# Other orders of work for layer 2 of a four-layer graph network kernel, on one core

## The reference

```python
qkv = (h @ W).reshape(Bn, Nn, 3, H, HEAD_DIM).transpose(2, 0, 3, 1, 4)
q, k, v = qkv[0], qkv[1], qkv[2]
mask = jnp.where(adj == 0, -jnp.inf, 0.0)
scores = jnp.einsum('bhid,bhjd->bhij', q, k) / np.sqrt(HEAD_DIM) + mask
out = jnp.einsum('bhij,bhjd->bhid', softmax(scores), v)
```

## Time and profile before

| | |
|---|---|
| median of 3 runs | 976.77 us (974.41 to 977.3) |
| the profiled execution's own time | 974.33 us |
| its span, first to last instruction | 972.3 us |
| TensorE busy | 904.8 us (93%) |
| VectorE, ScalarE, GpSimd busy | 641.8, 511.6, 382.1 us |
| mean granted TensorE clock | 0.965 of full speed |

### The profile page before, as it was taken

The page is one execution under the profiler, slowest core; times in us unless marked ns, Lnnn a source line. Parts: engine busy times, 40 slices in busy tenths (PEclk is TensorE's granted clock), DMA queues, the critical chain, the costliest instruction groups (busy, mean ns, idle before and its releaser), DMA issues. The chain is left out here.

```text
span 972.3 us, 20901 instructions
## 1 busy us (share of the span) xinstructions
PE 904.8 (93%) x6004; PEld 642.1 (66%) x6020; DVE 641.8 (66%) x1944; ACT 511.6 (53%) x919; POOL 382.1 (39%) x433
## 2 busy tenths in 40 slices
PE   6999999999999699976489999999999998999996
PEld 5799999999999688732255444455444443677775
DVE  4754554554554676556366777677776774899997
ACT  4323121121121336564356777777777757888884
POOL 4011021021020130000246777777777766355554
PEclk9999999999999899988579999999999999999999
DMA  8000000000000100000133343333343331011111
GB/s 243 23 12 12 12 23 12 11 22 11 22 0 0 35 9 0 0 1 1 33 66 66 67 90 86 81 69 65 67 92 81 84 77 25 1 33 32 32 32 43
DMA packets 34235, 40.66 MB, mean 42 GB/s; under 512 B 6672, under 2 KB 17552, under 8 KB 34192
## 3 DMA queue, kind: packets, MB, share of 16 engines
q1 hardware_dynamic: 32816, 39.87, 17.1%
q10 hardware_dynamic: 1376, 0.27, 0.1%
HBM read 6.43 MB, written 4.19 MB: 11 GB/s over the span
## 5 line engine op out<-in xcount | busy, mean ns | idle before, releaser
L1756 DVE CUSTOM_DVE_ANT_0 junk<-bank,mask_ij 128x512 bf16<-128x512 f32 x256 | 166.4, 688 | 69.2 <-PE bank L1839 61.1
L1617 POOL TENSOR_TENSOR half_sum<-prob 128x1024 f32<-128x1024 f32 x64 | 151.8, 2381 | 30.1 <-ACT prob L1692 29.9
L1692 ACT ACTIVATE prob<-wide 128x1024 f32<-128x1024 f32 x128 | 126.8, 1017 | 54.7 <-PE wide L1856 54.7
L431 ACT CAST yT<-wide 128x512 fp32r<-128x512 f32 x48 | 28.2, 589 | 206.1 <-PE wide L827 156.8
L531 POOL TENSOR_TENSOR Xr<-Xf,Xr 128x512 fp32r<-128x512 f32 x16 | 20.4, 1291 | 168.2 <-ACT Xr L426 167.9
L1839 PE MATMUL bank<-qkT 32*128 32x512 f32 x256 | 75.5, 513 | 6.6 <-DVE mx L1756 5.3
L1839 PEld LDWEIGHTS bank<-qkT 32*128 32x128 f32 x256 | 31.2, 187 | 70.8 <-DVE mx L1756 46.0
L1852 PE MATMUL wide<-qk_st 128*128 128x512 f32 x256 | 76.1, 419 | 0.0
L1439 PEld LDWEIGHTS bank<-Wh,pr 128*128 128x128 f32 x512 | 65.3, 191 | 13.7 <-ACT pr L1292 5.3
L59 PE MATMUL bank<-z,L3T_hi 128*128 128x256 f32 x256 | 73.9, 289 | 0.0
L60 PE MATMUL bank<-z,L3T_hi 128*128 128x256 f32 x256 | 73.6, 287 | 0.0
(11 more groups left out here) (299 smaller groups left out, 2285.3 us busy)
## 6 DMA issues: line engine op xcount, KB each, us to landing
qk_st<-qkT SPq DMA_DIRECT2D x192, 128.0 KB, 2.4
out_dram<-rc SPq DMA_DIRECT2D x15, 256.0 KB, 2.3
Xf<-X SPq DMA_DIRECT2D x14, 256.0 KB, 2.3
A<-in_adj_dram SPq DMA_DIRECT2D x4, 256.0 KB, 4.6
qk_st<-neg_row SPq DMA_DIRECT2D x64, 2.0 KB
Xf<-in_x_dram SPq DMA_DIRECT2D x2, 256.0 KB, 7.1
mask_q<-mask_ji SPq DMA_DIRECT2D x16, 32.0 KB, 1.8
w<-in_L_gnn_W_dram SPq DMA_DIRECT2D x2, 128.0 KB, 2.2
```

What stands on the lines that cost most here:

```text
L1617: pool.tensor_tensor(flat(half_sum[h][:]), flat(prob[bp][h][:, 0:2]), flat(prob[bp][h][:, 2:4]), ALU.add).then_inc(h_sum, 1)
L1692: act.activation(flat(prob[bp][h][:, 2 * half:2 * half + 2]), wide[half][:], ACT.Exp, scale=SCALE).then_inc(t_exp, 1)
L1756: dve.tensor_tensor_reduce(out=junk[hh][:], in0=bank[4 + hh][:], in1=m.mask_ij[:, i], scale=1.0, scalar=3.0 * MASKED, op0=ALU.add, op1=ALU ...
```

## The change

All five lists of layer 2 are replaced. The new lists begin at another place of the same cycle, so most stage numbers differ by one without the piece being done in another place. What stands elsewhere in the cycle is this:

- TensorE: before, `t0 D0 s0 m D1 V0 s1 t1 V1 s2 x V2 V3 s3 t2`; after, `t0 s0 m D0 D1 V0 V1 s1 t1 s2 V2 V3 s3 x t2`. T stands after s5 and ahead of q, no longer after t3.
- ScalarE: nr ahead of E4 and no longer behind it; kh behind vc and no longer ahead of it; N between mr and E1 and no longer behind E5.
- VectorE: R ahead of ql; u7 ahead of kl, where kl stood ahead of u7.
- GpSimd: r ahead of S2, where it stood behind it.
- SyncE: for a batch, dn1 st0 dn0 st1 dn3 dn2 st2 st3 without another batch's pieces between them; before, st0 of a batch stood ahead of st2 and st3 of the one before, and dn1 and dn0 behind st1.
- At the border to layer 3 the loops run a step further and the lists of `tail` begin that much later. TensorE's m.15 stands ahead of 3x.0 and D0.14, no longer between D0.14 and D1.14. GpSimd's constants and first copy come later in its order, and S3.14 stands ahead of r.13 (behind it before).

```diff
-        PE_ORDER = staged("V0:4 s1:2 t1:3 V1:4 s2:2 x:1 V2:4 V3:4 s3:2 t2:3 s4:2 n:2 d:4 o:4 s5:2 q:1 t3:3 T:0 s6:2 k:1 "
-                          "v:2 s7:2 t0:2 D0:3 s0:1 m:2 D1:3")
-        ACT_ORDER = staged("y:5 f:4 xh:1 xc:1 E4:3 nr:2 E5:3 N:0 qh:1 E6:3 E7:3 kh:1 vc:2 E0:2 mr:2 E1:2 e:3 Y:0 E2:2 E3:2")
-        DVE_ORDER = staged("u5:2 ql:1 R:0 u6:2 kl:1 u7:2 B:0 u0:1 b:4 u1:1 u2:1 u3:1 u4:1 c1:3 c2:3")
-        POOL_ORDER = staged("S3:3 g1:0 g2:4 S0:2 S1:2 xl:0 S2:2 r:3 X:0")
-        SP_ORDER = staged("st3:2 dn3:2 st1:1 dn1:1 dn0:1 st0:0 st2:1 dn2:1")
+        PE_ORDER = staged("t0:3 s0:2 m:3 D0:4 D1:4 V0:4 V1:4 s1:2 t1:3 s2:2 V2:4 V3:4 s3:2 x:1 t2:3 s4:2 n:2 d:4 o:4 "
+                          "s5:2 T:0 q:1 t3:3 s6:2 k:1 v:2 s7:2")
+        ACT_ORDER = staged("kh:2 E0:3 mr:3 N:0 E1:3 Y:1 e:4 E2:3 E3:3 y:5 f:4 xh:1 xc:1 nr:2 E4:3 E5:3 qh:1 E6:3 E7:3 vc:2")
+        DVE_ORDER = staged("u5:2 R:0 ql:1 u6:2 u7:2 kl:1 B:0 u0:1 b:4 u1:1 u2:1 u3:1 u4:1 c1:3 c2:3")
+        POOL_ORDER = staged("xl:1 r:4 S2:3 X:1 S3:3 g1:0 g2:4 S0:2 S1:2")
+        SP_ORDER = staged("st3:1 dn1:0 st0:0 dn0:0 st1:0 dn3:0 dn2:0 st2:0")
...
-            run(pool, POOL_ORDER, work, last=15)
+            run(pool, POOL_ORDER, work, last=16)
             third.pool_constants(pool)
-            tail("S3.13 g2.12", POOL_ORDER, work, None)
             third.pool_copy(pool, 0, 0, first=True)
-            tail("S0.14 S1.14 S2.14 r.13 S3.14 g2.13 S0.15 S1.15", POOL_ORDER, work, None)
+            tail("S2.14 S3.14 r.13 g2.13 S0.15 S1.15", POOL_ORDER, work, None)
...
-            run(act, ACT_ORDER, work, last=16)
+            run(act, ACT_ORDER, work, last=17)
             item = third.act_items(act)
-            tail("y.12 f.13 E4.14 nr.15 E5.14 E6.14 E7.14 vc.15 E0.15 3XR.0 mr.15 E1.15 3X.0 e.14 E2.15 E3.15 y.13 f.14 E4.15 "
...
+            tail("E0.15 3XR.0 mr.15 E1.15 3X.0 e.14 E2.15 E3.15 y.13 f.14 E4.15 E5.15 3W0.0 3W1.0 E6.15 E7.15 3XR.1 3G.0 3L0.0 "
...
-            run(pe, PE_ORDER, work, last=16)
+            run(pe, PE_ORDER, work, last=17)
             item = third.pe_items(pe)
             pe.wait_ge(third.const, 3)
-            tail("V0.13 s1.15 t1.14 V1.13 s2.15 V2.13 V3.13 s3.15 t2.14 s4.15 n.15 d.13 o.13 s5.15 t3.14 s6.15 v.15 s7.15 t0.15 "
-                 "3x.0 D0.14 m.15 D1.14 V0.14 t1.15 V1.14 3j.0 V2.14 V3.14 t2.15 d.14 o.14 3w0.0 3w1.0 t3.15 3i.0 3x.1 3j.1 D0.15 "
...
+            tail("t0.15 m.15 3x.0 D0.14 D1.14 V0.14 t1.15 V1.14 3j.0 V2.14 V3.14 t2.15 d.14 o.14 3w0.0 3w1.0 t3.15 3i.0 3x.1 3j.1 "
...
```

More of the change, by code:

```diff
@@ L1707, in work @@
                     act.copy(oT[:], ring["V0"][:]).then_inc(o_c, 1)
-            run(act, ACT_ORDER, work, last=16)
+            run(act, ACT_ORDER, work, last=17)
             item = third.act_items(act)
-            tail("y.12 f.13 E4.14 nr.15 E5.14 E6.14 E7.14 vc.15 E0.15 3XR.0 mr.15 E1.15 3X.0 e.14 E2.15 E3.15 y.13 f.14 E4.15 "
-                 "E5.15 3W0.0 3W1.0 E6.15 E7.15 3XR.1 3G.0 3L0.0 3L1.0 3X.1 3L2.0 e.15 3L3.0 y.14 3E0.0 f.15 3W0.1 3W1.1 3E1.0 "
-                 "3XR.2 3G.1 3L0.1 3L1.1 3X.2 3L2.1 y.15", ACT_ORDER, work, item)
+            tail("E0.15 3XR.0 mr.15 E1.15 3X.0 e.14 E2.15 E3.15 y.13 f.14 E4.15 E5.15 3W0.0 3W1.0 E6.15 E7.15 3XR.1 3G.0 3L0.0 "
+                 "3L1.0 3X.1 3L2.0 e.15 3L3.0 y.14 3E0.0 f.15 3W0.1 3W1.1 3E1.0 3XR.2 3G.1 3L0.1 3L1.1 3X.2 3L2.1 y.15", ACT_ORDER, work, item)
             pairs(act, B, 4, third.in_order(item, third.act_order), last=B, first=3)
@@ L1886, in work @@
                     last.then_inc(d_ps, 1)
-            run(pe, PE_ORDER, work, last=16)
+            run(pe, PE_ORDER, work, last=17)
             item = third.pe_items(pe)
             pe.wait_ge(third.const, 3)
-            tail("V0.13 s1.15 t1.14 V1.13 s2.15 V2.13 V3.13 s3.15 t2.14 s4.15 n.15 d.13 o.13 s5.15 t3.14 s6.15 v.15 s7.15 t0.15 "
-                 "3x.0 D0.14 m.15 D1.14 V0.14 t1.15 V1.14 3j.0 V2.14 V3.14 t2.15 d.14 o.14 3w0.0 3w1.0 t3.15 3i.0 3x.1 3j.1 D0.15 "
-                 "D1.15 V0.15 V1.15 V2.15 3q0.0 3q1.0 V3.15 3w0.1 3q2.0 3w1.1 3q3.0 d.15 o.15 3i.1 3x.2 3a0.0 3j.2 3a1.0 3q0.1 "
-                 "3q1.1 3a2.0", PE_ORDER, work, item)
+            tail("t0.15 m.15 3x.0 D0.14 D1.14 V0.14 t1.15 V1.14 3j.0 V2.14 V3.14 t2.15 d.14 o.14 3w0.0 3w1.0 t3.15 3i.0 3x.1 3j.1 "
+                 "D0.15 D1.15 V0.15 V1.15 V2.15 3q0.0 3q1.0 V3.15 3w0.1 3q2.0 3w1.1 3q3.0 d.15 o.15 3i.1 3x.2 3a0.0 3j.2 3a1.0 "
+                 "3q0.1 3q1.1 3a2.0", PE_ORDER, work, item)
             pairs(pe, B, 4, third.in_order(item, third.pe_order), first=3)
```

## The result

| | before | after |
|---|---|---|
| median, same chip | 976.73 us (974.41 to 977.3, 4 runs) | 970.62 us (969.82 to 971.99, 4 runs) |
| ratio with its 95% interval | | 0.9943 [0.9923, 0.9964] |
| the profiled execution's own time, span | 974.33, 972.3 us | 969.93, 968.0 us |
| mean granted TensorE clock | 0.965 | 0.965 |
| one step of the loop | 20.77 us | 20.44 us |

The account below looks back on a forecast made before the run. TensorE's sequence was taken to bound the kernel, at 20.77 us a step. Loop -2.1, fill -2.0 and border -0.1 summed to -4.2 us: 972.6 from a median of 976.8, range 968 to 978.

Parts of the forecast that it names:

- the loop: Layer 2's steady steps: -0.16 us a step over 13 steps, -2.1 us, bounds -3.4 to +1.8.
- the border: Where layer 3 begins: D0.14 and D1.14 joined, GpSimd's r.13 later; -0.1 us, between -0.3 and +0.5.
- the fill: Start of layer 2's pipeline: k no longer waits for ql, x moves behind s3; -2.0 us, between -0.6 and -3.
- Joined column tiles: TensorE's D0, D1, V0, V1 in one run: two junctions more at 0.12 us each, -0.24 us a step.
- The rival that joining saves nothing: Loads of all-row groups don't overlap, new neighbours bring nothing: step 21.0, total 977.7 us, no measurable change; chance 0.17.
- New neighbours of x and T: TensorE: t2 behind x saves 0.10 us a step, q behind T 0.05.
- Waits between scores and maxima: TensorE's score pairs waiting on VectorE: 0.36 us a step before, 0.54 after, +0.18.
- D0 behind kl: D0 follows k on its bank and waits for kl: covered by 0.07 us, +0.05 a step, bounds 0 and 0.2.
- GpSimd: r ahead of S2, X and S3 costs nothing, with 0.3 to 0.4 us of cover before D0 needs S3.
- The rival with a stall: GpSimd bounds the step because r ahead of S2 and S3 makes D0 wait: slower, above +2.9 us; chance 0.10.
- the third rival: The fill gives nothing because TensorE's clock falls again, and the loop alone pays: 974.1 us, about the same; chance 0.13.

Follow-up runs that it names:

- the split kernel: Changed kernel with D0 s0 m D1 V0 s1 t1 V1 ordered as before, each piece keeping the changed kernel's bank: 983.48 us, 1.0078 of the kernel before.
- the second pair: Both kernels executed once more with no edit: before 975.45 us (ratio 0.9994), after 971.22 us (ratio 0.996).

## Why the prediction was right, and which of its terms were off

The forecast lay 2 us above the median, on the right side of no change, and its range held the median. The mechanism in the loop was right. The sizes were not: the loop and the border gave 1.8 and 1.7 us more than forecast in the profiled execution, the fill 4.1 less, and these cancelled by luck.

*Joined column tiles*, forecast -0.24 us a step: measured 3.83 in before to 3.57, -0.26, and +0.27 when two junctions are taken away again. The rival that joining saves nothing is refuted. The weight loads show the overlap themselves: V0's first load runs at 642.24, while D1's last matmuls run until V0's first starts at 642.67.

```profile
642.24 0.14 PEld L1872 LDWEIGHTS bank<-prob,v 128*32 128x32 f32 x4 [0.29 <-issue]
```

(The Trainium skill, TensorE: Matmul & The Clock Gate, Part 3, The mechanism, lists that loads overlap matmuls in flight only where the row group differs, while its text ahead of the list also names a background weight buffer; the trace disagrees with the list for these all-row groups at different column tiles.)

*New neighbours of x and T*, forecast -0.10 and -0.05: this is the term of the step that was mis-sized. x took 0.59 us to V2, in front of all-row column tiles, and takes 0.41 in front of t2; t2 falls from 1.49 to 1.47. That is -0.20, and x put back costs it. T and q go from 0.59 + 0.81 to 0.53 + 0.80, -0.07 (653.69 to 654.22). I had looked for the saving in the full-height matmul behind the transpose, and it was in the transpose itself: what a piece takes to the next start depends on its successor as well. d, behind n, fell from 0.71 to 0.66, which wasn't forecast.

*Waits between scores and maxima*, forecast 0.36 to 0.54: measured 0.15 at s0, 0.16 at s2 and 0.29 at s5, 0.60 in all. s4 and s7 wait for nothing, as forecast. In every second step s7 takes 0.54 to 0.59 instead of 0.43, and then s0 waits less (0.43 to 0.49 instead of 0.59): one replaces the other. The body of the loop ends there, and s7 takes 0.43 where the loop is left, so I put it down to the loop's branch. That isn't shown: in before the body ends between D1 and V0, and D1 takes 0.88 to 0.89 in every step.

*D0 behind kl*, forecast +0.05: m to D0 goes from 0.20 to 0.27, +0.07. The bound of 0.2 wasn't reached, but the experiments show how near it is: with D0 a score pair and m earlier the wait is 0.66 us (the split kernel).

The step's sum, -0.26 - 0.20 - 0.07 - 0.05 + 0.24 + 0.07 = -0.27, comes within 0.06 of the measured -0.33. Averages over the loop's steps with complete records close the gap: the joined tiles give -0.28 (3.85 to 3.57), m to D0 +0.06, and v, which took 1.05 us in every second step of before and 0.98 in the others, takes 0.98 throughout: -0.03. Over the whole loop it is -3.93, where the forecast had -2.1: 1.8 us more, and outside the bounds given for it (-3.4 to +1.8).

*GpSimd*: the cover was forecast at 0.3 to 0.4 us and is 0.4. The rival with a stall never came near. Nor did t0 wait for a transfer in any step, and q (654.22) stood directly behind T; it waited for c2 once, 0.46 us at 776.88.

*The fill*, forecast -2.0. Its beginning went as forecast: counted from T of batch 0, s0 of batch 0 starts 1.85 us earlier (475.95 - 459.33 against 473.35 - 458.58; forecast 1.6) and t0 of batch 0 3.0 us. The term as a whole was borne out for the order itself (2.2 with the clock held up), and wrong for this execution (+1.4; -0.6 in the second pair; counted from T of batch 0, +2.1 and -0.2). That is the third rival's first half, TensorE's clock; the rival was too small in price, about 1.5 us, and I had argued that the new fill leaves no longer gap. It does: 1.90 us ahead of s1 of batch 1, where before's longest in the same place was 1.29. But closing that gap to 0.61 didn't keep the clock up, so the gap isn't the cause that it looks like. What is shown is that the clock costs the fill's gain; that adding matmuls brings it back; and that the clock is lower with this order than with before's: over 480 to 515 us it is 0.60 to 0.68 in the six traces whose fill has the new TensorE order, and 0.74 and 0.70 in before's two. Before loses by the clock too, only less: with the added matmuls t0 of batch 1 comes 4.3 to 6.0 us earlier in it, and 7.6 to 8.0 in after. (The Trainium skill, TensorE: Matmul & The Clock Gate, Part 1, HAM oscillation, tells of a kernel whose clock falls in waits for transfers and must be won back each time. Here the clock fell behind a wait for VectorE, but no run shows that the wait brought it down.)

*The border*, forecast -0.1: t0.15 to t3.15 goes from 13.27 to 12.95 us, -0.3, and about so in every other pair. The other -1.5 of the profiled pair lies in D0 and D1 of batch 15, behind the same waits, first before, then after:

```profile
822.73 3.40 PE L1864 MATMUL bank<-half_sum,ones_hd 128*32 128x512 f32 x16 [1.01 <-POOL half_sum L1617]
```

```profile
819.87 1.92 PE L1862 MATMUL bank<-half_sum,ones_hd 128*32 128x512 f32 x16 [1.00 <-POOL half_sum L1617]
```

Over the 10 us from there on the granted clock is 0.85 in before and 1.00 in after, but 0.72 and 0.85 in their second executions, where these matmuls take 3.64 and 3.35 us. The same order shows the fall once and once not, so I count the -1.5 as chance.

Open stays why the clock comes back at 500 us in the two traces with x ahead of V2 in the fill and only behind 505 us in those of the new order without it, and why it does so in some executions only. Before's fill has TensorE busy for only 2.59 of the 4 us from 496 to 500 and still has the full clock there, so a look at one gap doesn't settle it. Not tried: x early and the added matmuls together, and added matmuls at the border.

## What to carry to other kernels

Price a piece by the distance to the start of its successor and put it beside the successor it will have, not the one it had; a transpose that moved from in front of column tiles to in front of a full-height piece was worth 0.20 us a step here, more than a junction of two groups of column tiles (0.13). When an order is generated, work out anew what it implies (which pieces share a bank, what is read out behind what) for every edit, since two edits can be halves of one. And where a pipeline fills with TensorE partly idle, time the fill with the clock held up before judging an order by it: the clock was worth 7 us here, more than the whole change.

## What the runs showed of the hardware that was not expected

- In after's fill TensorE was busy for 3.53 of 4, 4.50 of 5 and 4.34 of 5 us (496 to 510 us), and the granted clock was 0.59 and then 0.50 up to 512 us. With 88 more matmuls it was 1.00 from 480 us on, and the whole kernel took 963.74 us against 970.62.
- A four-matmul transpose takes 0.41 us to the next start in front of t2 (full height), 0.53 in front of q, and 0.59 in front of column tiles or a 32-row pair; the profile shows no wait in any of these places.
- Where the loop's body ends, the last score pair takes 0.11 to 0.16 us longer in every second step of the changed kernel, and the wait that follows it is shorter by about as much. The branch as its cause is argued, not shown.
- Two executions of one unchanged kernel differ by 1.6 us in the start of the first dense step (1.2 of it behind T of batch 0), while the loop repeats to 0.01 us a step.
